# A graph network's tail: unit loads and stores issued by ScalarE, and a ring of 12 slots for the last visits

## What is computed

```python
# layer 0
m = silu(concat([x[src], x[dst], edge_attr]) @ msg_W1 + msg_b1) @ msg_W2 + msg_b2
agg = segment_sum(m, dst)
h = silu(concat([x, agg]) @ upd_W1 + upd_b1) @ upd_W2 + upd_b2
x = layernorm(x + layernorm(x + h) * gamma + beta)
# layer 1
agg = segment_sum(x[src], dst) / maximum(degree, 1)
h = relu(relu(concat([x, agg]) @ W1 + b1) @ W2 + b2)
x = layernorm(x + h)
```

## Time and profile before

| | |
|---|---|
| median of 3 runs | 2191.05 us (2190.15 to 2192.39) |
| the profiled execution | 2192.59 us |
| its span | 2190.8 us |
| PE / DVE / POOL / ACT busy | 90% / 74% / 69% / 64% |
| DMA | 487.73 MB, 223 GB/s over the span |
| mean granted clock of PE | 0.937 |

### The profile page before, as it was taken

The page is one execution under the profiler, slowest core; times in us unless marked ns, Lnnn a source line. Parts: engine busy times, 40 slices in busy tenths (PEclk is TensorE's granted clock), DMA queues, the critical chain, the costliest instruction groups (busy, mean ns, idle before and its releaser), DMA issues.

```text
span 2190.8 us, 58541 instructions
## 1 busy us (share of the span) xinstructions
PE 1967.6 (90%) x19638; PEld 1740.5 (79%) x19638; DVE 1631.8 (74%) x5459; ACT 1411.4 (64%) x3734; POOL 1519.4 (69%) x1605
## 2 busy tenths in 40 slices
PE   7898988988898998899899999899998999999686
PEld 7887777777786787787798797788898788999575
DVE  8697877877687877877777877878777878886343
ACT  3686766766586766776766766766766766775132
POOL 7477777777777777777777777777777777774010
PEclk9997988998998999998999999999999999999899
DMA  8476576685676686686788686787888687887775
GB/s 293 130 236 194 164 215 190 186 243 169 194 228 198 186 251 198 183 264 185 226 254 254 205 270 195 236 265 228 258 248 247 200 279 242 276 255 228 221 246 165
DMA packets 285033, 487.73 MB, mean 223 GB/s; under 512 B 118330, under 2 KB 143164, under 8 KB 284728
## 3 DMA queue, kind: packets, MB, share of 16 engines
q1 hardware_dynamic: 233278, 378.15, 55.0%
q0 software_dynamic: 50016, 102.53, 17.9%
q10 hardware_dynamic: 1434, 3.25, 0.4%
HBM read 375.62 MB, written 108.13 MB: 221 GB/s over the span
## 4 chain that ended last, share of the span: by engine, by line
POOL 53%; issue 25%; DMA 8%; PE 6%; DVE 5%; ACT 1%; DVEq 0%; SPq 0%; ACTq 0%; POOLq 0%
POOL gath L839 53%; DMA gath<-P_d,src_i 7%; PE ps_pre L1099 2%; DVE edgeK L898 1%; PE ps_cnt L1116 1%; DVE pre L911 1%; PE ps_p L382 1%; POOL sumT L846 1%; DVE edgeL L896 1%; PE ps_sum L1136 1%; PE ps_l L1152 0%; ACT counts L1255 0%; PE ps_pre L1101 0%; DMA Q_d<-Qst 0%; DMA A_d<-counts 0%
## 5 line engine op out<-in xcount | busy, mean ns | idle before, releaser
L839 POOL DMA_INDIRECT gath<-P_d,src_i x1535 | 1460.0, 951 | 490.8 <-issue 456.1
L898 DVE TENSOR_SCALAR edgeK<-iotaK,key 128x500 bf16<-128x500 f16 (+1 forms) x1564 | 666.6, 486 | 0.0
L1099 PE MATMUL ps_pre<-wc,eT_c 128*128 128x128 f32 x3128 | 618.5, 320 | 1.1 <-ACT gath L1266 1.1
L1116 PE MATMUL ps_cnt<-edgeK,edgeL 128*128 128x250 bf16 (+1 forms) x3128 | 487.7, 304 | 72.9 <-DVE edgeK L898 60.7
L911 DVE TENSOR_TENSOR pre<-ps_pre,gath 128x512 f32<-128x512 f32 x384 | 261.7, 681 | 363.6 <-DMA gath<-P_d,src_i 321.6
L1099 PEld LDWEIGHTS ps_pre<-wc,eT_c 128*128 128x128 f32 x3128 | 512.0, 205 | 24.0 <-issue 1.5
L1295 ACT ACTIVATE h<-pre 128x512 f32<-128x512 f32 x391 | 245.4, 628 | 431.4 <-DVE pre L911 424.2
L1136 PE MATMUL ps_sum<-edgeN,h 128*128 128x40 f32 x3128 | 421.4, 285 | 80.7 <-ACT h L1295 80.3
L1136 PEld LDWEIGHTS ps_sum<-edgeN,h 128*128 128x128 f32 x3128 | 392.0, 196 | 106.0 <-ACT h L1295 93.1
L1255 ACT ACTIVATE counts<-ps_cnt 128x1000 bf16<-128x1000 f32 x391 | 402.7, 1030 | 56.1 <-PE ps_cnt L1122 42.5
L1116 PEld LDWEIGHTS ps_cnt<-edgeK,edgeL 128*128 128x128 bf16 x3128 | 290.6, 102 | 144.9 <-DVE edgeK L898 72.5
(11 more groups left out here) (154 smaller groups left out, 1467.5 us busy)
## 6 DMA issues: line engine op xcount, KB each, us to landing
eT_c<-eT SPq DMA_DIRECT2D x196, 512.0 KB
A_d<-counts SPq DMA_DIRECT2D x168, 384.0 KB
rel_c<-rel_d SPq DMA_DIRECT2D x196, 240.0 KB
A_v<-A_d SPq DMA_DIRECT2D x85, 448.0 KB
gath<-P_d,src_i POOLq DMA_INDIRECT x1535
A_d<-counts SPq DMA_DIRECT2D x56, 416.0 KB
A_v<-A_d SPq DMA_DIRECT2D x87, 256.0 KB
Qw<-Q_d SPq DMA_DIRECT2D x56, 180.0 KB
```

The costliest lines, as they stand in the source:

```text
L839: pool.indirect_dma_start(gath[:, q, t * D:(t + 1) * D], None, v["P_d"], bass.IndirectOffsetOnAxis(ap=src_i[g % 2][:, c:c + 1], axis=0)).t ...
L898: last = V.tensor_scalar(edgeK[x][:, ROFF[j]:ROFF[j] + A2 * w], iotaK[j][:, :, 0:A2 * w // KR], key[k][:, q * QT + j:q * QT + j + 1], None ...
L1099: T.matmul(o, eT_c[c % RE][:, e0:e0 + P], wc[:], start=True, stop=False)
L1116: last = T.matmul(o[:, :, w0:w0 + w], edgeL[x][:, j, 0:P], r, start=(j == 0), stop=(j == QT - 1 and q == 0), skip_group_check=True)
```

## The change

Two things. First, `load_last` and `store_last` leave SP's program. ACT issues the first three `load_last` in step 402, after the layer 0 unit work of that step; the store of unit `w` and then the load of unit `w + 3` follow ACT's own line 1359 in step 6 of the unit, the store behind a wait for ACT's own `l_norm`. Second, the ring from step 396 on has 12 slots: six more lie in the two `counts` tiles, three in each, and their loads wait until all stores from that tile have landed (`c_out`). Visits from step 406 on are loaded ten steps ahead, but never before a load that stands earlier in the list (`plan_loads`).

```diff
-VB, RA, RT, LEAD = 14, 4, 6, 4
+VB, RA, RT, LEAD, AHEAD = 14, 4, 12, 4, 10
@@
+def plan_loads():
+
+    at, last = {}, 0
+    for i, (s, d, lo, hi) in enumerate(VISITS):
+        last = max(last, s - (AHEAD if s >= QUADS + AHEAD + LEAD else LEAD))
+        at.setdefault(last, []).append(i)
+    return at
+
+
+LOADS_AT = plan_loads()
@@
     A_v += [edgeK[k][:, 0:VB * P] for k in range(2)]
+    A_v += [counts[k][:].rearrange("p a d -> p (a d)")[:, j * VB * P:(j + 1) * VB * P] for k in range(2) for j in range(3)]
@@ load_visit
             if r >= RA:
                 sp.wait_ge(cnt_mm, NQ)
+            if r >= RA + 2:
+                sp.wait_ge(c_out[(r - RA - 2) // 3], 16 * len(PARTS) * (GROUPS // 2))
@@ sync, fast
-                if s + LEAD in VISIT_AT:
-                    load_visit(VISIT_AT[s + LEAD])
+                for i in LOADS_AT.get(s, ()):
+                    load_visit(i)
                 if s == GQ:
                     load_weights(nc, sp, v)
-                if s == UNITS[-1][2] + U_LEN + 1:
-                    for w in range(3):
-                        load_last(w)
-                store_last(s)
-                w = last_at(s, 4)
-                if w is not None and w + 3 < len(LAST_UNITS):
-                    load_last(w + 3)
@@ scalar, last_step
                 last.then_inc(l_norm, 1)
+                act.wait_ge(l_norm, w + 1)
+                act.dma_start(v["out"][last_columns(w)[0], :].rearrange("(j p) n -> p j n", p=P),
+                              z[:, 0:n, :]).then_inc(l_out[w % 3], 16)
+                if w + 3 < len(LAST_UNITS):
+                    load_last(w + 3)
@@ scalar, fast
                 unit_step(s)
+                if s == UNITS[-1][2] + U_LEN + 1:
+                    for w in range(3):
+                        load_last(w)
                 last_step(s)
```

More of the change, by code:

```diff
@@ L758, in unit_degrees @@
                 sp.dma_start(deg[:, cols], v["rdeg_d"][cols].partition_broadcast(P)).then_inc(dg_io, 16)
[L760 to L782, removed]
         def fast():
@@ L1333, in unit_step, with load_last @@
                 A.activation(xT1_u[:, 0:n * P], ps_u[:, 0:n * P], ACT.Copy).then_inc(u_xT, 1)
+        def load_last(w):
+            cols, n = last_columns(w)
+            r = w % 3
+            if w == 0:
+                act.wait_ge(pre_add, NQ)
+                act.wait_ge(x1_out, 16 * len(UNITS))
+                act.wait_ge(x1T_out, 16 * len(UNITS))
+            if w >= 3:
+                act.wait_ge(l_hidden, w - 2)
+                act.wait_ge(l_z, 2 * (w - 2))
+            act.dma_start(xT_l[r][:, 0:n * P], v["x1T_d"][:, cols]).then_inc(l_xT_in[r], 16)
+            act.dma_start(x_l[r].rearrange("p (j n) -> p j n", n=D)[:, 0:n, :],
+                          v["x1_d"][cols, :].rearrange("(j p) n -> p j n", p=P)).then_inc(l_x_in[r], 16)
         def last_step(s):
```

## The result

The changed kernel takes 2184.95 us, the median of 8 runs (2181.76 to 2189.34), against 2191.27 us for the kernel before in the same rounds (2188.44 to 2194.17). The ratio is 0.997, with a 95% interval of 0.996 to 0.9979: faster by 0.3%, 6.3 us by the medians and 4.6 to 8.8 us by the interval. The profiled execution took 2182.68 us, with a span of 2180.9 us.

What follows compares the result with a forecast made beforehand. PE was taken to bound the last 150 us, waiting for late loads until 2062 and then for DVE. Gap 3.56 plus clock 1.9 minus ACT 0.2 gives 5.2 us, from 2191.05 to 2185.8 us; range 2182 to 2191.3.

Steps and rivals of the forecast that it cites:

- What bounds the tail: Last 150 us: PE has most to do; it waits for loads until 2062, then only for DVE's add, 15.9 us.
- Part 1: Loads up to visit 200: no gain; the six A_v waits, 6.3 us, stay.
- Part 2: Visit 201's load goes out at about 2044.3, so PE's idle 3.56 us ahead of visit 201 goes.
- The step on what is late next: At unit 0's first matmul, line 1211: its xT load lands at 2053.5, before PE comes at 2055.2; wait taken as 0.
- The count of eleven loads ahead of it: By 2048.9 the loads of 199 to 209, 2528 KB, stand on SP's queue, and are through by 2051.
- Case (b): Rival: the wait moves to line 1211, xT landing 5.4 us later and PE waiting 3.3 us; 2191.0 us, chance 0.12.
- Part 3: TensorE's clock returns at about 2054, not 2061.6, speeding visit 201 and lines 1211 and 1213; 1.9 us gained.
- case (c): Rival: the low spell at 2068 and one more go too, 3.3 us beyond the sum; 2182.5 us, chance 0.13.
- Part 4: Wider ring behind visit 205: no gain; the waits there are truly for DVE, and no lead shortens their 15.9 us.
- Part 5: ACT's added issues, about 1.05 us in each of 13 units, are covered by its idle time; +0.2 us at the end.
- Case (d): Rival: ACT issues over 0.92 us delay each next unit's root; 2196.0 us at 1.2 us each; chance 0.07 with like losses.
- The sum: Whole kernel: 3.56 + 1.9 - 0.2 = 5.2 us less than the median of 2191.05, giving 2185.8 us.

Runs made afterwards that it cites:

- e4: The changed kernel with the late ring entered at free slots instead of slot 0; 2182.95 us, ratio 0.9960 to the kernel before.
- e1: The kernel before with only the ring of 12 and early loads; load_last and store_last stay on SP; 2186.06 us, ratio 0.9983.
- e2: The kernel before with only the move to ACT; ring of 6, loads 4 steps ahead; 2185.35 us, ratio 0.9973.
- e3: The kernel before with SP issuing the first three load_last in step 404, not 402; 2186.85 us, ratio 0.9979.
- e10: e8 with its 12 slots but a lead of 4 steps for every load; 2168.98 us, ratio 0.9893 to the kernel before.
- e5: The changed kernel with four PSUM banks for visits from step 402, so PE may be four visits ahead of DVE's add, not two; 2182.42 us, ratio 0.9954.
- e8: The changed kernel with free-slot ring entry, four PSUM banks, and last units but the final two starting four steps behind their last visit, not two; 2169.12 us.
- e12: e8 with a ring of 6 slots and a lead of 4, a repeat timing; 2164.17 us, ratio 0.9873 to the kernel before.
- e11: The kernel of e12 with load_last and store_last back on SP, in the steps of the kernel before; 2172.18 us, ratio 0.9919.

## Why the prediction was right, point by point

**What bounds the tail.** Right: PE's own work with waits, 9.9 us for loads before 2062 and 15.9 us for DVE behind. Of these waits visit 201's is the one that went.

**Part 1, nothing before visit 200.** Right: seven pieces on both sides, 7.4 us before (one of them, 1.0 us, put down to DVE) and 7.5 us after. That half of this was SP's stop for slot 0 (e4) I had read past: the plan gives 190 a tenant two steps back, and I noted only that its number stays.

**Part 2, the 3.56 us.** Right in size and cause; e1, e2 and e3 show the cause, since three unlike edits, which have in common that 201's load goes out ahead of the wait for the x1T store or past it, all give the gain. The step on what is late next held as well, by a small margin: xT of unit 0 was to land 4.6 us after its issue and took 5.2, and PE came 1.4 us after it had landed. In e1 PE came sooner and waited 1.02 us. The count of eleven loads ahead of it was too high. SP's issues took some 0.78 us each for 199 to 205 and not 0.38, so it was at the seventh when ACT issued the xT load at 2045.31; the estimate that 2528 KB would be through by 2051 falls with that count. Case (b)'s delay of 5.4 us did not come for the first load; the second and third were 4.2 and 7.0 us later than before, but were wanted later.

**Part 3, the clock.** The term was 1.9 us and the trace has 2.9 us from the first unit to the end of the units, of which 1.3 us is the first unit's pair (0.95 + 0.34, as worked out) and 1.5 us the second low spell, which is gone (0.95 us at its line 1211 and 0.6 at the next). On top of it visits 199 to 201 keep PE busy for 4.87 us and not 5.77 (2049.99 to 2053.78 and 1.98 us more), so 0.9 us less where I had 0.6 for 201 alone; visit 198 lost 0.3 of this, the clock having fallen sooner. The clock was back at about 2051.2 in the trace of after, which is 2054.3 in the time of the one before; I had said 2054. The second spell was the first half of case (c). e1 and e3 have it at 2.02 and 2.03 us, so the forecast was right to leave it out of the sum. How much of the clock's part is chance is open: there is one trace of the kernel before, and its 20.5 us at the low clock are the most of all.

**Part 4, the ring is worth nothing.** Right for this change: ten pieces and 15.9 us on both sides, and e2, without the ring, gives the same gain. Three things were missing behind it. I took the lead of ten steps as real; e10 shows that the slots set it. I did not see that a longer queue costs: landings of 12 and 13 us where the ring of 6 had 7.5. And that DVE is the releaser does not mean that freeing PE of it pays: in e5 the wait moved to POOL, with the units' start two steps behind.

**Part 5, ACT.** Right. Its issues took 0.46 us at the median for xT and 0.38 for the stores, some 1.3 us a unit and not 1.05, and its wait for the statistics is 45.0 us against 45.3: covered. The end is 0.19 us later, 0.2 in the sum. Case (d), issues over 0.92 us, did not come, though single ones reach 1.00 us here, 1.46 us in e8 and 1.93 us in e10.

**The sum.** 5.2 us forecast, 6.3 us measured by the medians, 6.8 us in the tails of the two traces. What the sum lacks against the traces, 1.6 us, is about the second low spell, and that was the luck of one trace. Against the medians it lacks 1.1 us, and their interval, 4.6 to 8.8 us, holds 5.2. The rule of the Trainium skill (DMA: Bandwidth & Descriptors, Issuing engines are not separate DMA queues), that another issuer saves issue time alone, gives too little here: the move alone was worth 6.0 us in e2, where the prediction had 2.5 us for the issues, and 8.0 us in e12 against e11. What counts besides is what stands behind a wait in the issuer's program, and e3 gets the same gain with one issuer.

## What to carry to other kernels

Where one engine issues all DMAs in program order, look in its queue for a wait that does not concern the transfers behind it, and ask which of them is the next to be missed; issuing three loads two steps later may be worth as much as a new ring. A lead counted in steps of the issuer's own loop is no lead in time: where nothing else in the loop waits, the slots decide how far it runs ahead, and the loads ahead can make a rare but urgent load land later. When a wait for an engine is put away, follow that engine's product to its other readers before the gain is counted.

## What the runs showed of the hardware

A queue of its own did not keep ACT's loads apart from SP's. The 13 xT loads of 256 KB landed after these times (us, minimum, median and maximum):

| | ring of 6 | ring of 12 |
|---|---|---|
| issued on SP | 2.7 / 3.3 / 4.9 (before) | 2.9 / 4.4 / 5.9 (e1) |
| issued on ACT | 3.5 / 5.3 / 6.4 (e2) | 4.3 / 6.1 / 11.9 (the change) |

The medians grow with the move and with the ring; each cell is one trace. In all 14 traces an xT load took more than 7.6 us only with both, where the longest took 11.7 to 13.1. The table doesn't say why the same load is faster on SP's queue; one thing that differs is that SP issues it behind the visits' loads, and ACT while SP is still issuing them.

The low clock is not tied to one idle time. After a wait of 2.6 to 3.1 us for DVE PE worked at 1.2 GHz at the second unit in the kernel before, in e1 and in e3, and after one of 3.08 us at 2.4 GHz in the changed kernel. In the 14 traces the low clock held for 0 to 20.5 us of the tail, up to PE's last matmul, so a single trace can be some microseconds off for that alone.
